# State-space stage joined to the block before it, with the router's logits taken from its output product

## What is computed

```python
h = tok(x)                         # attention over 16 frames, merged to 8: 2048 tokens x 192
h = h + mamba(layernorm(h))        # the state-space stage
h = h + experts8(layernorm(h))     # 8 experts, the best 2 of each token
h = h + linear_attention(layernorm(h))
h = h + experts3(layernorm(h))     # 3 experts, one for each sequence

# mamba, after u @ W_in, a causal convolution and silu:
h_t = exp(dt*A) * h + (dt * x_t) B_t ;  y_t = h_t C_t          # over the tokens, 6 heads of 64
y  = (y + D * xs)                                               # the skip
yg = y * silu(z)
yn = yg * rsqrt(mean(yg^2) + eps) * norm_w
out = yn @ W_out                                                # 384 -> 192

# experts8:
router_logits = layernorm(h) @ w_gate                           # 192 -> 8
top_p, top_i = top_k(softmax(router_logits), 2); top_p /= sum(top_p)
```

## Time and profile before

| | us |
|---|---|
| median of 3 runs | 552.89 (552.71 to 554.67) |
| the profiled execution | 552.83 |
| its span, first to last instruction | 550.7 |
| merge_frames and project_in | 0 to 122.3 |
| state_space | 122.6 to 200.8 |
| first DVE operation of pair_dispatch | 202.28 |
| first `up` of experts 1 | 221.81 |
| first `up` of experts 2 | 464.27 |

### The profile page before, as it was taken

The page is one execution under the profiler, slowest core; times in us unless marked ns, Lnnn a source line. Parts: engine busy times, 40 slices in busy tenths (PEclk is TensorE's granted clock), DMA queues, the critical chain, the costliest instruction groups (busy, mean ns, idle before and its releaser), DMA issues.

```text
span 550.7 us, 15738 instructions
## 1 busy us (share of the span) xinstructions
PE 503.6 (91%) x5797; PEld 460.2 (84%) x5797; DVE 367.9 (67%) x1045; ACT 258.1 (47%) x737; POOL 225.6 (41%) x327
## 2 busy tenths in 40 slices
PE   8999999988989845999999999999989997999993
PEld 7677777876778734999999999999878887999993
DVE  2676589966989978565666566564447765677671
ACT  2677868763544413333333333332357651645541
POOL 1244420002987833455455555543212224355522
PEclk9999999997999955999999999999999997999998
DMA  9992000008753100113131231220643323122210
GB/s 261 248 199 50 2 1 2 0 0 260 234 175 104 45 30 23 37 53 89 52 89 53 62 80 44 54 45 23 193 153 101 94 88 87 39 72 73 69 39 21
DMA packets 42877, 46.00 MB, mean 84 GB/s; under 512 B 7377, under 2 KB 38226, under 8 KB 42802
## 3 DMA queue, kind: packets, MB, share of 16 engines
q1 hardware_dynamic: 36082, 30.63, 20.6%
q0 software_dynamic: 5760, 12.98, 8.2%
q10 hardware_dynamic: 960, 1.38, 0.9%
HBM read 29.41 MB, written 10.32 MB: 72 GB/s over the span
## 4 chain that ended last, share of the span: by engine, by line
PE 55%; DVE 3%; issue 2%; ACT 2%; DMA 1%; POOLq 0%; POOL 0%; DVEq 0%; ACTq 0%
PE psum L1532 22%; PE psum L1544 20%; PE psum L1923 3%; PE psum L146 3%; PE psum L1514 2%; PE psum L1927 2%; PE psum L1934 1%; ACT rows_turned L1882 1%; PE psum L1680 1%; DVE hidden_room L1282 1%; PE psum L1915 1%; DMA rows_in<-y,token 1%; DVE token_in_tile_pairs L1287 0%; PE psum L1684 0%; PE psum L1689 0%
## 5 line engine op out<-in xcount | busy, mean ns | idle before, releaser
L1532 PE MATMUL psum<-rows_turned,expert_weights 64*128 64x128 f32 x2052 | 128.9, 277 | 0.0
L1544 PE MATMUL psum<-expert_second_weights,hidden_room 64*128 64x192 f32 x1368 | 121.0, 323 | 2.2 <-issue 2.2
L1532 PEld LDWEIGHTS psum<-rows_turned,expert_weights 64*128 64x128 f32 x2052 | 121.4, 191 | 0.3 <-issue 0.2
L1544 PEld LDWEIGHTS psum<-expert_second_weights,hidden_room 64*128 64x128 f32 x1368 | 110.1, 187 | 2.8 <-issue 2.8
L1496 POOL DMA_INDIRECT y<-rows_out,out_row_by_slot x39 | 45.2, 1160 | 73.7 <-DVE rows_out L1626 73.7
L1571 ACT ACTIVATE hidden_room<-psum 128x384 f32<-128x384 f32 x78 | 34.0, 488 | 64.0 <-PE psum L1532 64.0
L1624 DVE COPY rows_out<-psum 128x192 f32<-128x192 f32 x39 | 13.9, 358 | 57.8 <-PE psum L1544 57.8
L1489 POOL DMA_INDIRECT rows_in<-x,token x39 | 43.4, 1113 | 21.9 <-issue 11.6
L1557 ACT ACTIVATE rows_turned<-psum 128x192 f32<-128x192 f32 x57 | 18.9, 332 | 64.1 <-PE psum L1514 64.1
L786 PE MATMUL psum<-arena 97*128 97x512 f32 (+1 forms) x192 | 47.0, 400 | 1.1 <-ACT sz L813 0.5
L1569 ACT ACTIVATE hidden_room<-psum,expert_weights 128x128 f32<-128x128 f32 x108 | 29.9, 376 | 31.4 <-PE psum L1532 31.3
(11 more groups left out here) (278 smaller groups left out, 982.1 us busy)
## 6 DMA issues: line engine op xcount, KB each, us to landing
xbc_tile<-xbc SPq DMA_DIRECT2D x16, 320.0 KB, 3.4
w_proj<-in_w_proj SPq DMA_DIRECT2D x8, 576.0 KB, 5.5
sz<-in_x SPq DMA_DIRECT2D x16, 192.0 KB, 7.3
w_fc<-in_w_fc SPq DMA_DIRECT2D x4, 768.0 KB, 18.8
w<-in_w SPq DMA_DIRECT2D x3, 576.0 KB, 4.0
w_fc<-in_w_fc SPq DMA_DIRECT2D x4, 384.0 KB, 17.3
x<-xf_tile SPq DMA_DIRECT2D x16, 96.0 KB, 1.6
expert_rows<-y SPq DMA_DIRECT2D x8, 192.0 KB, 3.8
```

The source lines that it names most:

```text
L1532: done = nc.tensor.matmul(ps_h[t.odd][half][:, ch, :], w_now[at, t.odd, first:first + P], xt[at, t.odd, block, :], start=block == 0 and ch ...
L1544: done = nc.tensor.matmul(ps_y[half], hid[at, t.odd, ch, :], w_down_now[at, t.odd, ch * D:(ch + 1) * D], start=ch == 0, stop=ch == HC - 1)
```

## The change

`state_space` no longer makes a block. It returns its engines' parts as functions, which `merge_frames` calls at the end of its own block, so no barrier stands between; the rows of x, B and C are read where they are (`s.xbc`) and the `xbc_tile` copies are gone; all steps are written out, 25 instead of 27; `ps_d`, `ps_g` and `ps_x` get two banks each; 14 fillers stand between the first two tiles' `decay_and_bc`, in place of the 28 at the projection's end; the x1 stores are awaited by the gather of experts 1.

The logits come another way. `w_out` gets eight more columns, w_out times the centred gate weights, so that `project_out` yields 200 columns, and `h` has eight columns beside its 192 for `h` times the centred gate weights, which `merge_frames` fills. `residual` adds all 200. `max` and `max_index` read `m.h` and write whole rows of eight; `turn`, `take_turned`, `route`, `take_logits`, `keep_top` and `keep_index` are gone. The logits lack the row's 1/std, which does not change the order; `pair_dispatch` multiplies it in. The norm of x1 is on ScalarE, its shift on DVE (`set_shift`), eps on ScalarE, and POOL takes the mean square's root of tile *i* and the variance's of tile *i*−2 as one `pow`. In `experts`, `up` stands before `turn_rows`.

```diff
@@ merge_frames, PE
+                def gate_through_w_out(t):
+                    if t.i == 0:
+                        pe.wait_ge(m.w_out_loaded, 16)
+                    if t.i < 2:
+                        for ch in range(3):
+                            last = nc.tensor.transpose(ps_wo[t.i][:, ch, :], m.w_out[:, ch, t.i * HD:(t.i + 1) * HD], c["ident"])
+                        last.then_inc(wo_turned, 1)
+                    if t.i == 3:
+                        pe.wait_ge(dt_ready, 5)
+                        for ch in range(3):
+                            for half in range(2):
+                                last = nc.tensor.matmul(ps_wog[:, ch, :], wo_t[:, half, ch, :], m.w_gate[:, half, :], start=half == 0, stop=half == 1)
+                        last.then_inc(wog_mm, 1)
@@ steps
-                    need(pe, dt_out, t.i)
+                    need(pe, logits_out, t.i)
@@ the block's PE end
-                pe.wait_ge(dt_out, TILES)
+                pe.wait_ge(logits_out, TILES)
                 projection.chunk(pe, 0, 7)
                 projection.tensor(pe)
+                mixing.tensor(pe)
@@ merge_frames, ACT
+                def take_logits(t):
+                    act.wait_ge(dt_out, t.i + 1)
+                    act.wait_ge(ratio_set, t.i + 1)
+                    act.activation(m.h[:, t.i, D:], ps_dt[:, NH:], ACT.Identity, scale=ratio[:, t.i % 4:t.i % 4 + 1]).then_inc(logits_out, 1)
@@ project_in, PE
-        pe.wait_ge(taps_done, 3 * (5 * (STRETCHES - 1) + 1))
-        stay_busy(nc, banks[0][:, 0:P], m.c["ident"], 28)
@@ state_space, PE
+            if t.i == 0:
+                pe.wait_ge(projection.taps_done, 3 * 17)
+            elif t.i == 1:
+                pe.wait_ge(projection.gate_out, 12)
+                stay_busy(nc, ps[:, 7, 256:256 + P], c["ident"], 14)
-                pipelined(pe, TILES, [(6, add_squares), (3, mix_time), (9, turn), (10, route), (5, project_out), (1, decay_and_bc)], 12)
+        pipelined(pe, TILES, [(6, add_squares), (3, mix_time), (5, project_out), (1, decay_and_bc)], 7, straight=True)
@@ state_space, ACT
+                act.activation(under[:, t.odd, 1:2], mv[:, i % 4, 1:2], ACT.Identity, bias=c["eps"]).then_inc(eps_done, 1)
+                act.wait_ge(shift_set, i + 1)
+                act.activation(xf[:, odd, :], row(i), ACT.Identity, bias=shift2[:, odd:odd + 1], scale=rms[:, t.i, 1:2]).then_inc(xf_done, 1)
-                pipelined(act, TILES, [(2, decays), (5, squares), (9, take_turned), (3, skips)], 12)
+        pipelined(act, TILES + MS_TO_VAR, [(2, decays), (6, with_eps), (5, squares), (3, skips), (7, norm)], 8, straight=True)
@@ state_space, DVE
+            nc.vector.scalar_tensor_tensor(m.h[:, t.i, :], ps_o[t.odd], rms[:, t.i, 0:1], m.h[:, t.i, :], ALU.mult, ALU.add).then_inc(h_done, 1)
+            nc.vector.max(m.top[:, t.i, :], m.h[:, t.i, D:R]).then_inc(best_set, 1)
+            nc.vector.tensor_scalar(shift2[:, t.odd:t.odd + 1], mv[:, t.i % 4, 0:1], rms[:, t.i + MS_TO_VAR, 1:2], -1.0, ALU.mult, ALU.mult).then_inc(shift_set, 1)
@@ state_space, POOL
+            nc.gpsimd.tensor_tensor(rms[:, t.i, at], under[:, t.odd, at], c["minus_half"].to_broadcast([P, at.stop - at.start]), ALU.pow).then_inc(roots_done, 1)
@@ pair_dispatch, DVE
+        then(nc.vector.tensor_copy(pick[:, :, :], m.pick[:, :, 0:2]))
+        nc.vector.tensor_tensor(m.gate[:, :, 1], m.gate[:, :, 0], m.roots2[:, MS_TO_VAR:, 1], ALU.mult).then_inc(gate_set, 1)
@@ experts, PE
-        pipelined(pe, n_tiles, [(1, turn_rows), (2, up), (3, down)], 4, straight=True)
+        pipelined(pe, n_tiles, [(2, up), (1, turn_rows), (3, down)], 4, straight=True)
```

More of the change, by code:

```diff
@@ L44 @@
 QKV = 3 * D + 1 + 2 * E2
+MS_TO_VAR = 2
 SPARE = T1 - 2 * N_TOK // P
@@ L130, in need @@
         eng.wait_ge(sem, value)
-def need_alone(eng, m, *counts):
-    counts = [(sem, value if isinstance(value, int) else eng.snap(value)) for sem, value in counts]
-    if not all(isinstance(value, int) for _, value in counts):
-        eng.wait_ge(m.loaded, 16)
-    for sem, value in counts:
-        need(eng, sem, value)
 def stay_busy(nc, to, of, count):
@@ L349, in semaphore, with merge_frames @@
         return self.semaphores[-1]
-def merge_frames(nc, dram, m, s, banks, projection):
+def merge_frames(nc, dram, m, s, banks, projection, mixing):
     with ExitStack() as ctx:
```

508 lines of the change are left out of this document (259 added, 249 removed).

## The result

The changed kernel has a median of 562.51 us (561.77 to 563.79, 4 runs) against 552.9 of the kernel before; the ratio is 1.0169, with a 95% interval of 1.014 to 1.0198. The prediction was 537.3 us, 533.5 to 543, and faster. The profiled execution took 562.9 us with a span of 561.0.

A forecast was written before the change was run, and what follows sets the result against it. VectorE was taken to set the state-space stage's pace, TensorE close behind. Merge and projection +3.1, state-space −17.7, dispatch +0.4, experts 1 −0.4, experts 2 −0.9: −15.5 from 552.83 gives 537.3 us, range 533.5 to 543.

The forecast's parts named there:

- The step that failed: Expert stages, steady part: putting up ahead of the turn costs 0, as TensorE is never idle in either order.
- the ramp: State-space stage, first to eighth mixing: without the copies VectorE's own work decides, 19.6 us against 22.3, gain 2.7.
- the drain: State-space stage's end: the logits' relay is gone, dispatch begins about 14.5 us after the last mixing.
- merge_frames: Stages before state-space: extra small products and turns, logits taken by ScalarE, later dt_exp; together +3.1 us, 1.8 to 4.5.
- the steady steps: State-space stage, eighth to last mixing: 3.70 us a step (3.61 to 3.90), 29.6 for eight, gain 3.8.
- The slower rival: State-space stage: TensorE runs at 1.2 GHz throughout and sets the pace; 561 us, slower than before, chance 0.03.
- The start of the expert stages: Dispatch chain +0.4 us; first up sooner, −0.4 in experts 1 and −0.9 in experts 2.
- Head of the stage: State-space start: without the barrier the table load follows the last silu; first mixing at 120.85, 6.3 us earlier.
- Rival 1: State-space stage's first tiles: TensorE's clock falls to 1.2 GHz, losing 1.5 to 2.5 us; 539.3 us, chance 0.16.
- Rival 2: State-space steps: the relay between ScalarE and GpSimd becomes the bound, near 4.0 us a step; 540.9 us, chance 0.12.
- Rival 3: merge_frames: TensorE waits 0.35 us for ScalarE's logits in each of 16 tiles, +5.3; 542.6 us, chance 0.09.

The follow-up runs named there:

- e1: The changed kernel with turn_rows ahead of up again in both expert stages; 539.81 us, ratio 0.9705 to the kernel before.
- e7: e1 with the state-space functions in a block of their own again, behind a barrier; 549.20 us, ratio 0.994 to the kernel before.
- e9: e1 without the 14 fillers between the first two tiles' products of the state-space stage; 543.96 us, ratio 0.986 to the kernel before.
- e8: e1 with the norm of x1 on VectorE in set_shift's place; 543.18 us, ratio 0.9836 to the kernel before.

## Why the prediction was wrong

**The step that failed** is one clause of the sum: "In the steady state PE is never idle in either order: 0." I read that TensorE was busy without a gap in the order of before and took it for a property of the stage. It is a property of the order: the turn stood two products ahead of the `up` that needs it. The trace of before held all the rest: the copy's two halves and the down behind them give the new order about 1 us of room, a sum that I did not make since I had no doubt. What the trace of before did not show is the 1.4 us lag that fills this room; in it GpSimd's DMAs lie behind the turn. The term measured 17.7 and 7.2 us in the two expert stages where I had 0 (1.9 of the 17.7 lie between the first two `up`), and e1 shows that without the new order the forecast's sum is near: 539.8 against 537.3, inside the range. Some of that nearness is luck, since the ramp, the drain and merge_frames came out longer and the steady steps shorter than forecast, and the kernel before took 552.9 us beside the changed kernel and 555.7 beside e1. No rival had the late copy in every tile; ACT's copy coming late stands in the prediction for the second up of experts 2 only, as a bound of +1.2. The slower rival that I did name (TensorE at 1.2 GHz all through the state-space stage) did not happen; the product takes 0.88 us there. That its 561 us lie near the measured 562.5 is an accident.

**The start of the expert stages.** The earlier trace rows for experts 1 became this, with up now straight behind the fillers:

```profile
208.21 0.40 PE L1547 MATMUL psum<-const,rows_twice 64*128 64x64 f32 x6 [0.49 <-DVE rows_twice L1650]
208.54 0.94 PE L137 MATMUL psum<-const 128*128 128x128 f32 x6
209.40 2.28 PE L1565 MATMUL psum<-rows_turned,expert_weights 64*128 64x128 f32 x36
```

The first `up` came 18.75 us after the dispatch began, 19.53 before: −0.8, and −1.6 beside e1 (20.40). I had +0.4 − 0.4. But the second `up` waits 1.70 us for ScalarE's copy and comes 4.16 us after the first instead of 2.29, so that by then nothing is left of the gain: 22.91 us after the dispatch began, 22.69 in e1. In experts 2 the first began 2.2 us sooner after experts 1 and ran at full clock (467.41, 2.28 us), and the second waited 2.25 us and took 3.91 us.

**Head of the stage: right in its number, wrong in one reason.** The last silu ends at 123.00, the table load follows at once, and the first mixing is 1.76 us behind the silu (1.83 forecast). The wait of 3.57 us of the earlier trace rows, which I put down to the barrier, was that of TensorE's fillers in front of it (until 122.33); both are gone. The earlier trace rows has become 124.76 and 145.24.

```profile
121.09 1.91 ACT L876 ACTIVATE xbc<-conv_out 128x512 f32<-128x512 f32 x3
123.02 1.28 ACT L1060 ACT_TABLE_LOAD   x1
124.31 0.20 ACT L1060 ACTIVATE exp_warm<-const 128x1 f32<-128x1 f32 x1
```

The load starts 0.02 us after the silu and work follows at once, so the drain that the Trainium skill's page "ScalarE: Activation LUTs" (section "What ACT_TABLE_LOAD costs") adds is not seen on the path either. e7 has a barrier without those fillers, and its load waits 0.27 us.

**Ramp**: 20.5 us (124.76 to 145.24), 19.6 forecast. Rival 1, the clock's dip, did not happen, and e9 shows that it would have without the fillers.

**Steady steps: mis-sized, to the good.** 3.51 us, below the 3.61 that I had as the lower bound, and 28.5 us for the eight against 29.6 forecast. Against 4.00 the step lost 0.49 where the spacings give 0.50 removed. `set_shift` adds nothing one can see: its 0.12 stands where other spacings shrank. One step, from mixing to mixing, which answers the earlier trace rows:

```profile
159.68 0.94 DVE L1111 TENSOR_TENSOR mix<-decays,bc_masked 128x768 f32<-128x768 f32 x1
...
161.13 0.21 DVE L1156 TENSOR_SCALAR minus_mean_times_root<-bn_mean_var,roots_by_step 128x1 f32<-128x1 f32 x1
...
163.19 0.95 DVE L1111 TENSOR_TENSOR mix<-decays,bc_masked 128x768 f32<-128x768 f32 x1
```

Rival 2, the relay over ScalarE and GpSimd, did not bound the step. e8 adds that the norm's move was worth more than its spacing in the earlier trace rows, 0.68 us and not 0.19.

**Drain: mis-sized.** From the last mixing (173.72) to the dispatch (190.65) 16.9 us, 14.5 forecast. The last residual came 10.95 us after the last mixing (184.67; 9.9 forecast), since DVE now waits for GpSimd's joint root (1.06 us at 183.38, the residual before it). From it to the last norm's end (188.72) 4.05 us (3.2 forecast): the norm waited 0.74 us for the store of the rows two tiles ago, a wait for which I had looked at the gather's side only.

```profile
183.38 0.43 DVE L1133 SCALAR_TENSOR_TENSOR h<-psum,roots_by_step,h 128x200 f32<-128x200 f32 x1 [1.06 <-POOL roots_by_step L1178]
...
188.17 0.55 ACT L1092 ACTIVATE xf_tile<-h,minus_mean_times_root,roots_by_step 128x192 f32<-128x192 f32 x1 [0.74 <-DMA x<-xf_tile]
...
190.65 0.51 DVE L1284 CAST picked_experts_pairs<-best_logits_index 128x32 f32<-128x32 uint32 x1 [3.13 <-PEq L165]
```

The barrier after it took 1.9 us (1.45 forecast). **merge_frames** cost 4.0 us in this execution (+3.1 forecast, 1.8 to 4.5); in the profiled executions of the other kernels with the same code the last silu ends between 121.0 and 123.8, so the term lies between 2.0 and 4.8 us and the forecast is inside. Rival 3, a wait in each tile, is not seen: between 25 and 75 us TensorE waits for ScalarE 0.7 us in all. From the last silu to the dispatch the change gave 15.6 us of the 17.7 forecast, within its bounds.

## What to carry to other kernels

That an engine is never idle says nothing about another order of its work: for each product that is moved, count the time from the step that feeds it, through the other engine's copy, to its new place, and ask how much of it is left as room. Keep the step whose result goes through another engine as far ahead as the buffers allow, above all where GpSimd issues DMAs in the same loop, because signals can come over a microsecond late there. A term that is put at 0 because an engine is busy in either case, and that stands for 57 repetitions, wants a check as much as the large terms do.

## What the runs showed of the hardware

- With GpSimd issuing gathers and scatters (records of 0.95 to 1.54 us), TensorE's semaphore signals arrived up to 1.6 us late in the changed kernel, while TensorE itself went on. The turn's came 0.24 to 0.49 us after the end of a gather's record; most of up's 0.9 us after the end of a scatter's, in the midst of the gather's. Signals of VectorE and DMAs arrived meanwhile (one of VectorE's at 281.02), and those of VectorE's and ScalarE's operations beside them came 0.01 us after their ends. A plain GpSimd sum of 0.83 us in the same place had no such effect, nor had a store from SyncE's queue.
- The transfers do not delay them: 56 signals of down came on time (0.03 us at most) while packets of GpSimd's queue were moving.
- Not every issue delays every signal: in the kernel before, the signals of up came 0.13 and 0.08 us ahead of the end of the scatter's issue (293.46 and 293.51 against 293.59) and were on time. What decides it stays open.
- GpSimd took 0.74 us from TensorE's signal to the issue of a gather that waited for it.
- A GpSimd root of two columns took 0.79 us in one arrangement and 1.42 in another, its second sum of squares 1.12 and 0.46, and VectorE's mixing 0.97 and 1.18, by which of the two GpSimd operations mixing met in the step.
